# Quantizing a layer-normed tile: one int8 round trip replaced by an int32 conversion, its remainder and a correction

## The chip, the cores and the metric

The kernel runs on all 8 cores of one Trainium2 chip. Each core takes one of the eight sequences (2048 tokens of 1024 features) and does the whole layer on it; the cores exchange nothing. The metric is the device time of the slowest core, in microseconds.

## The reference, cut to what matters

One transformer layer with the norms behind the blocks: an attention block whose weights are 1 + s + s²/2 under a causal mask, normalised by their sum, a residual and a layer norm, and then a linear layer that quantizes its input by row:

```
x = layernorm(x + attn(x, Wq, Wk, Wv, Wo))
amax    = max(|x|, axis=-1);  x_scale = max(amax, 1e-6) / 127
x_q     = clip(round(x / x_scale), -128, 127)            # int8
acc     = x_q @ weight_q.T                               # int32
out     = acc * x_scale * weight_scale + bias
x = layernorm(x + out)
```

The part of this document is the line that makes x_q.

## The kernel before, in words

The program is written by hand as one instruction stream per engine, in program order: a wait list, the instruction, a semaphore increment. Each engine runs its stream in order, so the order of the loops in the code is the order on the engine.

The stages of a core, one behind the other:

- Projections. TensorE makes q, k and v from the transposed input and the weights (L235, L289), VectorE moves them out of PSUM (L248, L298).
- Attention, by pairs of heads: TensorE's scores (L442), ScalarE's square (L462), VectorE's added half and mask (L470 to L485), TensorE's product with v (L505), and the division by the row sums (L375, L394).
- Output projection, residual and statistics, by 16 tiles of 128 tokens (L597 to L620). The result stays in SBUF as `x1`, 128 x (16 * 1024) f32; mean, variance, minimum and maximum of each token go to small columns of `stat`. A run of small VectorE operations turns them into `S2` and `MM2`, the factor and offset that take a row of `x1` to quantized units, and `V1` and `NMR`, which take it to the layer norm's output.
- Quantization, a loop over the 16 tiles, the stage that the diff touches. Per tile:
  - VectorE: `mk1` (L702) writes `t6 = x1 * S2 + MM2` in f32; `mk2a` (L709) copies it to `xq8`, int8, which rounds it; `mk2b` (L716) copies that to `xq`, f16. `t6`, `xq8` and `xq` have two buffers each. L709 waits for L702, L716 for L709 and for the transposes of two tiles before.
  - GpSimd: `mkxm` (L721) replaces the tile of `x1` by its normed value, and `mkx1b` (L736) adds the bias to it. L721 waits for this tile's L702, L736 for L721.
  - TensorE: eight 128x128 transposes (L746) of `xq` into PSUM, which wait for L716.
  - ScalarE: one copy (L756) of them into `xqT`.
- The quantized matmuls, a second loop over the 16 tiles: sixteen matmuls each (L777) on `xqT` and the weights, then VectorE's scaling (L788) and residual with row sum (L795), and ScalarE's sum of squares (L804). As the second loop stands behind the first in the program, TensorE's matmuls stand behind all its transposes, and L788 behind all of the quantization on VectorE.
- The second layer norm and the stores (L835), which use `t6` again as a staging buffer.

The rounding of the quantization happens in the conversion from f32 to an integer type; the integers are then carried as f16, in which they are exact.

Of the kernel before, what the change touches and what calls it, by code (L numbers as in the profile page):

```python
# [9 lines left out]
I8 = mybir.dt.int8  # L10
AF = mybir.ActivationFunctionType
ALU = mybir.AluOpType
# [4 lines left out]
D = 1024  # L17
# [10 lines left out]
MAGIC = 12582912.0  # L28
# [65 lines left out]
def build_nc(debug=False, _waits=None):  # L94
    if _waits is None:
        _waits = _collect_waits(debug)
    return _build_nc_inner(debug, _waits)


def _collect_waits(debug):  # L100
    nc, plan = _build_nc_inner(debug, {}, collect_only=True)
    return {k: sorted(v) for k, v in plan.waited.items()}


def _build_nc_inner(debug, _waits, collect_only=False):
    nc = bass.Bass("TRN2", target_bir_lowering=False,
                   dynamic_dma_scratch_size=8192)
# [33 lines left out]
    sDV = Sem(e(nc.semaphore("sDV")), "sDV")  # L141
# [44 lines left out]
    plan = Plan(nc, last_wait)  # L186
    plan.future_waits = _waits

    for dst, src in ((wsb, d_wsb), (biasb, d_biasb), (tri, d_tri),
                     (ident, d_ident), (ones2, d_ones2)):  # L190
        plan.op("sync", lambda sy, dst=dst, src=src: sy.dma_start(dst[:, :], src),
                incs=[(sIO, 16)])
# [8 lines left out]
    for fi in range(NCH):  # L201
# [3 lines left out]
                incs=[(sCa, 16)])  # L205
# [3 lines left out]
                incs=[(sCa, 16)])  # L209
# [9 lines left out]
    for proj in range(2):  # L219
        for c in range(NCH):  # L220
# [6 lines left out]
            for fi in range(NCH):  # L227
                waits = [(sCa, dma_after[(proj, fi)])]
                if prev in evac_dv:
                    waits.append((sDV, evac_dv[prev]))  # L230
                for qcc in range(QC):
# [5 lines left out]
                    incs = ()  # L237
                    if qcc == QC - 1 and (c == NCH - 1 or fi == NCH - 1):
                        incs = [(sPE, 1)]
                    plan.op("tensor", mk, waits=waits if qcc == 0 else (),  # L240
                            incs=incs)
# [5 lines left out]
            def mkev(v, ps=ps, dst=dst, scale=scale, c=c):  # L247
# [3 lines left out]
                    incs=[(sDV, 1)])  # L251
            evac_dv[(proj, c)] = sDV.n
        nxt = d_wkt if proj == 0 else d_wvt
        for fi in range(NCH):
# [4 lines left out]
                    waits=[(sPE, w_last_use[(proj, fi)])],  # L259
                    incs=[(sCa, 16)])  # L260
# [8 lines left out]
           for i in range(2)]  # L269

    plan.op("vector", lambda v: v.memset(vz_blocks[:, :, 64:65], 1.0),
            incs=[(sDV, 1)])

    v_evac = {}
    for t in range(NT):
# [6 lines left out]
        for fi in range(NCH):  # L282
            waits = [(sCa, dma_after[(2, fi)])] + extra
            extra = []
            for half in range(2):
# [5 lines left out]
                incs = [(sPE, 1)] if (fi == NCH - 1 and half == 1) else ()  # L291
                plan.op("tensor", mk, waits=waits if half == 0 else (), incs=incs)
                waits = ()
# [9 lines left out]
    if debug:  # L303
        plan.op("sync", lambda sy: sy.dma_start(d_qto, qT[:, :]),
                waits=[(sDV, n_qk_evac)], incs=[(sIO, 16)])
        plan.op("sync", lambda sy: sy.dma_start(d_kto, kT[:, :]),
                waits=[(sDV, n_qk_evac)], incs=[(sIO, 16)])
        plan.op("sync", lambda sy: sy.dma_start(d_vzo, vz[:, :]),
                waits=[(sDV, n_vz_done)], incs=[(sIO, 16)])
# [18 lines left out]
    for fi in range(NCH):  # L328
# [4 lines left out]
                incs=[(sCa, 16)])  # L333
# [80 lines left out]
    for p in range(NP):  # L414
# [128 lines left out]
        if p > 0:  # L543
# [3 lines left out]
                waits=wio, incs=[(sIO, 16)])  # L547
        gather_done[p] = sIO.n
        if debug and p == 0:
            plan.op("sync", lambda sy: sy.dma_start(d_oso, ot_sb[0][:, :]),  # L550
                    incs=[(sIO, 16)])
# [20 lines left out]
    if debug:  # L572
        plan.op("sync", lambda sy: sy.dma_start(d_oto, ot_fin[:, :]),
                waits=list(w_all), incs=[(sIO, 16)])

    r1_done = {}
    for t in range(NT):
        wio = []
        if t >= 2:
            wio.append((sDV, r1_done[t - 2]))  # L580
        plan.op("sync",
                lambda sy, t=t: sy.dma_start(xstream[t % 2][:, :],
                                             d_xtok[t * 128:(t + 1) * 128, :]),
                waits=wio, incs=[(sIO, 16)])
# [7 lines left out]
        for fi in range(NCH):  # L592
            for half in range(2):
# [5 lines left out]
                incs = [(sPE, 1)] if (fi == NCH - 1 and half == 1) else ()  # L599
# [11 lines left out]
        def mksq1(s, t=t):  # L611
# [3 lines left out]
                incs=[(sSc, 1)])  # L615
# [3 lines left out]
        def mkmn(v, t=t):  # L619
# [6 lines left out]
            waits=[(sDV, r1_done[NT - 1])], incs=[(sDV, 1)])  # L626
    plan.op("vector", lambda v: v.tensor_scalar(V1, SQ1, INV1024, None, ALU.mult),
            waits=[(sSc, n_sq1)], incs=[(sDV, 1)])
    plan.op("vector", lambda v: v.tensor_tensor(MSQ, M1, M1, ALU.mult),
            waits=[(sDV, sDV.n)], incs=[(sDV, 1)])  # L630
    plan.op("vector", lambda v: v.tensor_tensor(V1, V1, MSQ, ALU.subtract),
            waits=[(sDV, sDV.n)], incs=[(sDV, 1)])
    plan.op("scalar", lambda s: s.activation(V1, V1, AF.Sqrt, bias=c_eps),
            waits=[(sDV, sDV.n)], incs=[(sSc, 1)])
    plan.op("vector", lambda v: v.reciprocal(V1, V1),
            waits=[(sSc, sSc.n)], incs=[(sDV, 1)])
# [3 lines left out]
            waits=[(sDV, n_rstd1)], incs=[(sDV, 1)])  # L640
    plan.op("vector", lambda v: v.tensor_tensor(MN, M1, MN, ALU.subtract),
            waits=[(sDV, sDV.n)], incs=[(sDV, 1)])
    plan.op("vector", lambda v: v.tensor_tensor(MX, MX, MN, ALU.max),
            waits=[(sDV, sDV.n)], incs=[(sDV, 1)])
    plan.op("vector", lambda v: v.tensor_tensor(AM, MX, V1, ALU.mult),
            waits=[(sDV, sDV.n)], incs=[(sDV, 1)])
    plan.op("vector",
            lambda v: v.tensor_scalar(XS, AM, 1e-6, INV127, ALU.max, ALU.mult),
            waits=[(sDV, sDV.n)], incs=[(sDV, 1)])
    plan.op("vector", lambda v: v.reciprocal(RQ, XS),  # L650
            waits=[(sDV, sDV.n)], incs=[(sDV, 1)])
    plan.op("vector", lambda v: v.tensor_tensor(S2, V1, RQ, ALU.mult),
            waits=[(sDV, sDV.n)], incs=[(sDV, 1)])
    plan.op("vector", lambda v: v.tensor_tensor(MM2, M1, S2, ALU.mult),
            waits=[(sDV, sDV.n)], incs=[(sDV, 1)])
    plan.op("vector",
            lambda v: v.tensor_scalar(MM2, MM2, -1.0, None, ALU.mult),
            waits=[(sDV, sDV.n)], incs=[(sDV, 1)])
    plan.op("vector", lambda v: v.tensor_tensor(NMR, M1, V1, ALU.mult),
            waits=[(sDV, sDV.n)], incs=[(sDV, 1)])  # L660
    plan.op("vector",
            lambda v: v.tensor_scalar(NMR, NMR, -1.0, None, ALU.mult),
            waits=[(sDV, sDV.n)], incs=[(sDV, 1)])
# [5 lines left out]
    ef = scope_f.enter_context  # L669
    wqf = ef(nc.sbuf_tensor("wqf", [128, NCH * D], F16))  # L670
    xqT = ef(nc.sbuf_tensor("xqT", [128, NCH * T], F16))
    xq = [ef(nc.sbuf_tensor(f"xq{i}", [128, D], F16)) for i in range(2)]
    t6 = [ef(nc.sbuf_tensor(f"t6{i}", [128, D], F32)) for i in range(2)]
    xq8 = [ef(nc.sbuf_tensor(f"xq8{i}", [128, D], I8)) for i in range(2)]
    t3 = [ef(nc.sbuf_tensor(f"t3{i}", [128, D], F32)) for i in range(2)]

    ph4_psum = contextlib.ExitStack()
# [5 lines left out]
    for fi in range(NCH):  # L683
# [3 lines left out]
                waits=[(sDV, div_done[NP - 1]), (sIO, obmove_done[NP - 1])]  # L687
                if fi == 0 else (),
                incs=[(sCa, 16)])
    n_wq = sCa.n  # L690

    rnd1_done = {}
# [4 lines left out]
    for t in range(NT):  # L697
        wv = [(sDV, n_qscale)]
        if t >= 2:
            wv.append((sDV, rnd2_done[t - 2]))  # L700
        def mk1(v, t=t):
            return v.tensor_scalar(t6[t % 2][:, :], x1[:, t * D:(t + 1) * D],  # L702
                                   S2[:, t:t + 1], MM2[:, t:t + 1],
                                   ALU.mult, ALU.add)
        plan.op("vector", mk1, waits=wv, incs=[(sDV, 1)])
        rnd1_done[t] = sDV.n

        def mk2a(v, t=t):
            return v.tensor_copy(xq8[t % 2][:, :], t6[t % 2][:, :])  # L709
        plan.op("vector", mk2a, waits=[(sDV, rnd1_done[t]), (sDV, sDV.n)],  # L710
                incs=[(sDV, 1)])
        wv = [(sDV, sDV.n)]
        if t >= 2:
            wv.append((sPE, tr_done[t - 2]))
        def mk2b(v, t=t):
            return v.tensor_copy(xq[t % 2][:, :], xq8[t % 2][:, :])  # L716
        plan.op("vector", mk2b, waits=wv, incs=[(sDV, 1)])
        rnd2_done[t] = sDV.n

        def mkxm(g, t=t):  # L720
            return g.tensor_scalar(x1[:, t * D:(t + 1) * D],  # L721
                                   x1[:, t * D:(t + 1) * D],
                                   V1[:, t:t + 1], NMR[:, t:t + 1],
                                   ALU.mult, ALU.add)
        plan.op("gpsimd", mkxm, waits=[(sDV, rnd1_done[t])], incs=[(sPo, 1)])
        n_xm = (sPo, sPo.n)
        if debug:
            plan.op("sync",
                    lambda sy, t=t: sy.dma_start(d_x1o[t * 128:(t + 1) * 128, :],
                                                 x1[:, t * D:(t + 1) * D]),  # L730
                    waits=[n_xm], incs=[(sIO, 16)])
        wx1b = [n_xm, (sIO, n_const)]
        if debug:
            wx1b.append((sIO, sIO.n))
        def mkx1b(g, t=t):
            return g.tensor_tensor(x1[:, t * D:(t + 1) * D],  # L736
                                   x1[:, t * D:(t + 1) * D], biasb[:, :], ALU.add)
        plan.op("gpsimd", mkx1b, waits=wx1b, incs=[(sPo, 1)])
        x1b_done[t] = sPo.n

        wpe = [(sDV, rnd2_done[t]), (sIO, n_const)]
        if t >= 2:
            wpe.append((sSc, trevac_done[t - 2]))
        for c in range(NCH):
            def mktr(tt, t=t, c=c):
                return tt.transpose(pst[t % 2][:, c * 128:(c + 1) * 128],  # L746
                                    xq[t % 2][:, c * 128:(c + 1) * 128],
                                    ident[:, :])
            plan.op("tensor", mktr, waits=wpe if c == 0 else (),
                    incs=[(sPE, 1)] if c == NCH - 1 else ())  # L750
            wpe = ()
        tr_done[t] = sPE.n
        def mktre(s, t=t):
            src = pst[t % 2].rearrange("p (c b) -> p c b", b=128)
            dst = xqT.rearrange("p (c u) -> p c u", u=T)[:, :, t * 128:(t + 1) * 128]
            return s.copy(dst, src)  # L756
        plan.op("scalar", mktre, waits=[(sPE, tr_done[t])], incs=[(sSc, 1)])
        trevac_done[t] = sSc.n

    if debug:  # L760
        plan.op("sync", lambda sy: sy.dma_start(d_xqo, xqT[:, :]),
                waits=[(sSc, trevac_done[NT - 1])], incs=[(sIO, 16)])
# [3 lines left out]
    for t in range(NT):  # L766
# [5 lines left out]
        for fi in range(NCH):  # L772
            for half in range(2):
# [5 lines left out]
                incs = [(sPE, 1)] if (fi == NCH - 1 and half == 1) else ()  # L779
# [14 lines left out]
        def mkr2(v, t=t):  # L794
# [5 lines left out]
                incs=[(sDV, 1)])  # L800
        r2_done[t] = sDV.n

        def mksq2(s, t=t):
# [3 lines left out]
                incs=[(sSc, 1)])  # L807
    n_sq2 = sSc.n

    if debug:  # L810
        plan.op("sync", lambda sy: sy.dma_start(d_r2o, x1[:, :]),
                waits=[(sDV, r2_done[NT - 1])], incs=[(sIO, 16)])

    plan.op("vector", lambda v: v.tensor_scalar(M1, S1, INV1024, None, ALU.mult),
            waits=[(sDV, r2_done[NT - 1])], incs=[(sDV, 1)])
    plan.op("vector", lambda v: v.tensor_scalar(V1, SQ1, INV1024, None, ALU.mult),
            waits=[(sSc, n_sq2)], incs=[(sDV, 1)])
    plan.op("vector", lambda v: v.tensor_tensor(MSQ, M1, M1, ALU.mult),
            waits=[(sDV, sDV.n)], incs=[(sDV, 1)])
    plan.op("vector", lambda v: v.tensor_tensor(V1, V1, MSQ, ALU.subtract),  # L820
            waits=[(sDV, sDV.n)], incs=[(sDV, 1)])
    plan.op("scalar", lambda s: s.activation(V1, V1, AF.Sqrt, bias=c_eps),
            waits=[(sDV, sDV.n)], incs=[(sSc, 1)])
    plan.op("vector", lambda v: v.reciprocal(V1, V1),
            waits=[(sSc, sSc.n)], incs=[(sDV, 1)])
# [4 lines left out]
    for t in range(NT):  # L830
# [3 lines left out]
        def mka2(v, t=t):  # L834
# [6 lines left out]
                lambda sy, t=t: sy.dma_start(d_out[t * 128:(t + 1) * 128, :],  # L841
                                             ostage[t % 4][:, :]),
                waits=[(sDV, na)], incs=[(sIO, 16)])
# [56 lines left out]
```

How the kernel before makes its waits and increments, by code:

```python
        def thunk(eng, wl=wl, builder=builder, incs=tuple(incs)):  # L74
            for s, v in wl:
                eng.wait_ge(s.h, v)
            inst = builder(eng)
            for s, k in incs:
                inst = inst.then_inc(s.h, k)
```

## Time and profile before

| | us |
|---|---|
| median of 13 runs | 946.97 |
| lowest and highest of them | 944.14, 982.76 |
| the profiled execution, its own time | 949.38 |
| its span on the slowest core (core 3) | 947.8 |
| spans of the eight cores | 931.6 to 947.8 |
| busy in that span: TensorE matmul | 617.3 |
| VectorE | 480.4 |
| ScalarE | 376.3 |
| GpSimd | 102.5 |

The page is of one execution, on its slowest core. The time is measured from outside and is a little longer than the span from first to last instruction. In the trace PE is TensorE, DVE is VectorE, ACT is ScalarE, POOL is GpSimd and SP the engine that issues most transfers. A line such as L702 is the line in the kernel that issued the instruction. Tensors are shown without their buffer numbers, and without digits at the end of their names: `t6` and `t3` are both t, `x1` is x, and `xq8` and `xq` both read xq, so that the line number tells them apart. The duration of an instruction in the records runs from its start to its end and can hold time in which it was held up.

### The profile page before, as it was taken

The page shows a single profiled execution, that of the slowest core. Times are in us where ns is not written, and L with a number is a line of the kernel's source. Part 1 is how long each engine was busy: PE and PEld are TensorE (multiplying, and loading weights), DVE is VectorE, ACT ScalarE, POOL GpSimd, SP SyncE. Part 2 cuts the span into 40 slices and gives each one's busy share as a digit, 9 for nine tenths or more (in the row PEclk, how much of TensorE's full clock was granted, in tenths as well). Part 3 has the DMA queues.
Part 4 walks back from the last instruction along what each step waited for, and adds up shares of the span by engine and source line. Part 5 has one row for each costly group of instructions (what it writes and reads, how often), then busy time and mean ns, then how long its engine had stood idle before and what let it go on. Part 6 is the DMA issues. An engine that isn't in the chain of part 4 may idle for free.

```text
span 947.8 us, 8730 instructions; the slowest of 8 cores (931.6 to 947.8 us)
## 1 busy us (share of the span) xinstructions
PE 617.3 (65%) x2688; PEld 222.2 (23%) x2688; DVE 480.4 (51%) x761; ACT 376.3 (40%) x403; POOL 102.5 (11%) x100
## 2 busy tenths in 40 slices
PE   1239948945997787878787778787089611259900
PEld 0014413411442221212222222222034211124400
DVE  0002202221334566665656665656359999967742
ACT  0000000000008987978797979788013311213300
POOL 1100010012000000000000000000010078850000
PEclk9999968975998989988989988889589955569955
DMA  6550040035100011110111110101164300000035
GB/s 113 101 98 1 12 66 12 1 56 87 35 1 1 0 25 34 25 34 24 34 25 34 25 34 24 34 25 34 46 192 152 111 1 0 0 1 1 0 133 221
DMA packets 14831, 43.87 MB, mean 46 GB/s; under 512 B 2244, under 2 KB 2756, under 8 KB 13764
## 3 DMA queue, kind: packets, MB, share of 16 engines
q0 software_dynamic: 8192, 23.07, 12.7%
q1 hardware_dynamic: 6596, 20.25, 6.5%
q8 instruction: 23, 0.38, 0.2%
q14 instruction: 20, 0.16, 0.1%
HBM read 44.11 MB, written 8.52 MB: 56 GB/s over the span
## 4 chain that ended last, share of the span: by engine, by line
PE 34%; DMA 23%; DVE 17%; ACT 15%; issue 9%; POOL 0%; DVEq 0%; ACTq 0%; POOLq 0%; SPq 0%
ACT uab L462 15%; PE pq L235 10%; PE oab L505 8%; PE pa L777 6%; DMA wbuf<-wqt 6%; PE pv L289 6%; DMA xs<-x_tok 6%; DVE t L702 4%; PE ps L442 4%; DMA wbuf<-wvt 3%; DMA wbuf<-wkt 3%; DVE xq L716 2%; DVE uab L470 2%; DVE ot_fin L375 2%; DMA out<-xs 2%
## 5 line engine op out<-in xcount | busy, mean ns | idle before, releaser
L462 ACT ACTIVATE uab<-ps,consts 128x1024 f16<-128x1024 f32 (+1 forms) x320 | 321.4, 1085 | 55.5 <-PE ps L442 55.5
L505 PE MATMUL oab<-uab,vz 128*65 128x512 f16 (+3 forms) x640 | 194.2, 388 | 62.4 <-DVE uab L485 31.3
L235 PE MATMUL pq<-xTsb,wbuf 128*128 128x512 f16 x512 | 127.6, 412 | 70.5 <-DMA wbuf<-wqt 53.6
L442 PE MATMUL ps<-qT,kT 64*128 64x512 f16 (+3 forms) x640 | 124.7, 386 | 22.9 <-ACT uab L462 20.9
L485 DVE TENSOR_SCALAR uab<-uab 128x1024 f16<-128x1024 f16 x192 | 79.4, 422 | 105.0 <-ACT uab L462 105.0
L462 ACT ACT_TABLE_LOAD x1 | 1.3, 1283 | 284.4 <-PE ps L442 284.4
L235 PEld LDWEIGHTS pq<-xTsb,wbuf 128*128 128x128 f16 x512 | 51.5, 103 | 146.1 <-issue 94.7
L505 PEld LDWEIGHTS oab<-uab,vz 128*65 128x65 f16 x640 | 48.1, 116 | 144.1 <-issue 143.2
L597 PE MATMUL py<-woT,ot_fin 128*128 128x512 f16 x256 | 59.3, 389 | 27.5 <-DMA ot_fin<-ob_tmp 25.6
L289 PE MATMUL pv<-wbuf,xTsb 128*128 128x512 f16 x256 | 61.0, 400 | 23.3 <-DMA wbuf<-wvt 20.8
L470 DVE SCALAR_TENSOR_TENSOR uab<-uab,tri_sb 128x256 f16<-128x256 f16 x128 | 54.5, 426 | 42.6 <-ACT uab L462 41.1
L442 PEld LDWEIGHTS ps<-qT,kT 64*128 64x128 f16 x640 | 34.8, 94 | 154.4 <-issue 153.7
L248 DVE TENSOR_SCALAR qT<-pq 128x2048 f16<-128x2048 f32 x8 | 18.3, 2292 | 101.6 <-PE pq L235 101.6
L746 PE MATMUL pt<-ident_sb,xq 128*128 128x128 f16 x128 | 16.2, 307 | 76.2 <-DVE xq L716 76.2
L777 PE MATMUL pa<-wqf,xqT 128*128 128x512 f16 x256 | 57.6, 389 | 0.0
L298 DVE CAST vz<-pv 128x1024 f16<-128x1024 f32 x16 | 19.6, 1225 | 62.5 <-PE pv L289 62.5
L248 DVE TENSOR_SCALAR kT<-pq 128x2048 f16<-128x2048 f32 x8 | 18.3, 2292 | 61.0 <-PE pq L235 61.0
L612 ACT ACTIVATE scratch<-x 128x1024 f32<-128x1024 f32 x16 | 16.9, 1058 | 74.1 <-DVE x L605 74.1
L756 ACT COPY xqT<-pt 128x1024 f16<-128x1024 f16 x16 | 16.2, 1013 | 70.3 <-PE pt L746 70.3
L702 DVE TENSOR_SCALAR t<-x,stat 128x1024 f32<-128x1024 f32 x16 | 43.2, 2698 | 0.1
L736 POOL TENSOR_TENSOR x<-x,biasb_sb 128x1024 f32<-128x1024 f32 x16 | 41.5, 2593 | 2.4
L524 DVE COPY otsb<-oab 65x1024 f32<-65x1024 f32 x32 | 38.9, 1214 | 4.2 <-PE oab L505 4.2
(63 smaller groups left out, 401.7 us busy)
## 6 DMA issues: line engine op xcount, KB each, us to landing
rzb<-rzscr POOLq DMA_DIRECT2D x16, 512.0 KB, 4.7
xs<-x_tok SPq DMA_DIRECT2D x16, 512.0 KB
xTsb<-xT POOLq DMA_DIRECT2D x8, 512.0 KB, 5.6
out<-xs SPq DMA_DIRECT2D x8, 512.0 KB
out<-t SPq DMA_DIRECT2D x8, 512.0 KB
wbuf<-wqt POOLq DMA_DIRECT2D x8, 256.0 KB, 6.3
wbuf<-wkt POOLq DMA_DIRECT2D x8, 256.0 KB, 3.6
wbuf<-wvt POOLq DMA_DIRECT2D x8, 256.0 KB, 3.6
```

Source lines behind the costliest of these rows:

```text
L235: return t.matmul(ps[:, qcc * 512:(qcc + 1) * 512], lhs, rhs, start=(fi == 0), stop=(fi == NCH - 1))
L289: return tt.matmul(ps[:, half * 512:(half + 1) * 512], lhs, rhs, start=(fi == 0), stop=(fi == NCH - 1))
L442: return t.matmul(ps[:, ab * 512 + js: ab * 512 + 512], lhs, rhs, start=True, stop=True, tile_position=(r0, 0))
L462: return s.activation(dst, src, AF.Square, bias=c_rs, scale=c_rs)
L470: return v.scalar_tensor_tensor(ub[:, :, js:js + 128], ub[:, :, js:js + 128], 0.5, tri[:, None, :].broadcast_to([128, 2, 128]), ALU.add, A ...
L485: return v.tensor_scalar(ub[:, :, :], ub[:, :, :], 0.5, None, ALU.add)
L505: return t.matmul(ob[0:65, ab * 512 + js: ab * 512 + 512], lhs, rhs, start=(kt == 0), stop=(kt == 4 * qc + 3))
L524: return v.tensor_copy(dst, src)
L597: return tt.matmul(ps[:, half * 512:(half + 1) * 512], lhs, rhs, start=(fi == 0), stop=(fi == NCH - 1))
L702: return v.tensor_scalar(t6[t % 2][:, :], x1[:, t * D:(t + 1) * D], S2[:, t:t + 1], MM2[:, t:t + 1], ALU.mult, ALU.add)
L736: return g.tensor_tensor(x1[:, t * D:(t + 1) * D], x1[:, t * D:(t + 1) * D], biasb[:, :], ALU.add)
L777: return tt.matmul(ps[:, half * 512:(half + 1) * 512], lhs, rhs, start=(fi == 0), stop=(fi == NCH - 1))
```

## The change

In the quantization loop `mk2a`, the copy from f32 to int8, goes, and five operations take its place; `mk2b` becomes an addition. `mkc` converts `t6` to int32 (`xq32`). `mke` subtracts that integer from `t6`, in place, which leaves the remainder. `mkm1` and `mkm2` add a large constant to the remainder and take it off again, two separate operations in f32, which rounds it to a whole number. `mkg` doubles that and writes it as int32 over the same bytes (`g32` is `t6` seen as int32). The new `mk2b` adds `xq32` and `g32` and writes the sum as f16. Each of the six waits for VectorE's semaphore count of the one before it; the wait for the transposes of two tiles before stays at `mk2b`. The buffer `xq8` (2 x 1 KB per partition) becomes `xq32` (2 x 4 KB). The streams of the other engines are not edited, and the bounds of the int8 type no longer clip.

```
+    xq32 = [ef(nc.sbuf_tensor(f"xq32{i}", [128, D], mybir.dt.int32))
+            for i in range(2)]
+    er = t6
+    g32 = [b[:, :].bitcast(mybir.dt.int32) for b in er]
...
-        def mk2a(v, t=t):
-            return v.tensor_copy(xq8[t % 2][:, :], t6[t % 2][:, :])
-        plan.op("vector", mk2a, waits=[(sDV, rnd1_done[t]), (sDV, sDV.n)],
+        def mkc(v, t=t):
+            return v.tensor_copy(xq32[t % 2][:, :], t6[t % 2][:, :])
+        plan.op("vector", mkc, waits=[(sDV, rnd1_done[t]), (sDV, sDV.n)],
                 incs=[(sDV, 1)])
+        def mke(v, t=t):
+            return v.tensor_tensor(t6[t % 2][:, :], t6[t % 2][:, :],
+                                   xq32[t % 2][:, :], ALU.subtract)
+        plan.op("vector", mke, waits=[(sDV, sDV.n)], incs=[(sDV, 1)])
+        def mkm1(v, t=t):
+            return v.tensor_scalar(er[t % 2][:, :], er[t % 2][:, :],
+                                   MAGIC, None, ALU.add)
+        plan.op("vector", mkm1, waits=[(sDV, sDV.n)], incs=[(sDV, 1)])
+        def mkm2(v, t=t):
+            return v.tensor_scalar(er[t % 2][:, :], er[t % 2][:, :],
+                                   -MAGIC, None, ALU.add)
+        plan.op("vector", mkm2, waits=[(sDV, sDV.n)], incs=[(sDV, 1)])
+        def mkg(v, t=t):
+            return v.tensor_scalar(g32[t % 2], er[t % 2][:, :],
+                                   2.0, None, ALU.mult)
+        plan.op("vector", mkg, waits=[(sDV, sDV.n)], incs=[(sDV, 1)])
...
         def mk2b(v, t=t):
-            return v.tensor_copy(xq[t % 2][:, :], xq8[t % 2][:, :])
+            return v.tensor_tensor(xq[t % 2][:, :], xq32[t % 2][:, :],
+                                   g32[t % 2], ALU.add)
```

## Rows read from the trace of the kernel before

**Rows 1.** The page's chain that ended last, its shares of the span by line.
```profile
ACT uab L462 15%; PE pq L235 10%; PE oab L505 8%; PE pa L777 6%; DMA wbuf<-wqt 6%; PE pv L289 6%; DMA xs<-x_tok 6%; DVE t L702 4%; PE ps L442 4%; DMA wbuf<-wvt 3%; DMA wbuf<-wkt 3%; DVE xq L716 2%; DVE uab L470 2%; DVE ot_fin L375 2%; DMA out<-xs 2%
```
**Rows 2.** The chain in order of time, 836 to 906 us: start, length, what.
```profile
840.09 1.45 DVE xq L716
...
841.78 1.01 PE pt L746 x8
842.80 57.44 PE pa L777 x256
```
**Rows 3.** Busy time by stretch: length, PE, PEld, DVE, ACT, POOL, clock, DMA share, GB/s.
```profile
761.00:842.80 81.80, 16.19 (x129) 12.61 (x130) 76.28 (x48) 15.20 (x15) 67.51 (x32) 0.50 0.00 1
842.80:860.00 17.20, 17.20 (x71) 7.35 (x70) 8.66 (x10) 4.47 (x7) 0.93 (x1) 0.88 0.00 0
```
**Rows 4.** TensorE by stretch, 842 to 854 us: length, busy, clock, DMA share, GB/s.
```profile
846.00:847.00 1.00, 1.00 (x4) 0.50 0.00 0
847.00:848.00 1.00, 1.00 (x6) 0.97 0.00 0
```
**Rows 5.** The timeline, the first tiles of quantization: start, duration, engine, line.
```profile
761.00 0.81 DVE L702 TENSOR_SCALAR t<-x,stat 128x1024 f32<-128x1024 f32 x1
...
764.14 2.82 DVE L702 TENSOR_SCALAR t<-x,stat 128x1024 f32<-128x1024 f32 x1
...
767.07 0.69 DVE L709 CAST xq<-t 128x1024 int8<-128x1024 f32 x1
767.14 1.69 POOL L721 TENSOR_SCALAR x<-x,stat 128x1024 f32<-128x1024 f32 x1 [0.73 <-DVE t L702]
767.86 1.51 DVE L716 CAST xq<-xq 128x1024 f16<-128x1024 int8 x1
768.98 2.59 POOL L736 TENSOR_TENSOR x<-x,biasb_sb 128x1024 f32<-128x1024 f32 x1
769.29 2.82 DVE L702 TENSOR_SCALAR t<-x,stat 128x1024 f32<-128x1024 f32 x1
...
773.09 1.44 DVE L716 CAST xq<-xq 128x1024 f16<-128x1024 int8 x1 [0.17 <-DVE xq L709]
```
**Rows 6.** Instructions of line L716: count, then shortest, median, longest duration in ns.
```profile
L716 DVE CAST xq<-xq x16: 1437/1441/1509, 762.7 to 840.1; 128x1024 f16<-128x1024 int8 x16
```
**Rows 7.** Groups by line and shape, 640 to 948 us: count, busy us, mean ns.
```profile
L709 DVE CAST xq<-t 128x1024 int8<-128x1024 f32 x16 | 11.1, 694 | 1.6
L375 DVE TENSOR_TENSOR ot_fin<-otsb,rzb 64x512 f16<-64x512 f32 x8 | 5.0, 678 | 7.3 <-DMA rzb<-rzscr 7.3
L795 DVE SCALAR_TENSOR_TENSOR x<-t,x 128x1024 f32<-128x1024 f32 x16 | 19.6, 1226 | 2.8 <-DVE t L788 2.8
L485 DVE TENSOR_SCALAR uab<-uab 128x1024 f16<-128x1024 f16 x12 | 4.8, 419 | 6.3 <-ACT uab L462 6.3
```
**Rows 8.** Waits, 761 to 843 us: us in total, times, longest.
```profile
PE pt L746 <- DVE xq L716: 76.2, 16, 14.0
POOL x L721 <- DVE t L702: 72.0, 16, 61.1
```
**Rows 9.** The page's costliest groups, two of VectorE's that read PSUM.
```profile
L248 DVE TENSOR_SCALAR qT<-pq 128x2048 f16<-128x2048 f32 x8 | 18.3, 2292 | 101.6 <-PE pq L235 101.6
...
L298 DVE CAST vz<-pv 128x1024 f16<-128x1024 f32 x16 | 19.6, 1225 | 62.5 <-PE pv L289 62.5
```
**Rows 10.** The timeline, the last tile of quantization and the first residual.
```profile
836.30 2.82 DVE L702 TENSOR_SCALAR t<-x,stat 128x1024 f32<-128x1024 f32 x1
...
840.09 1.44 DVE L716 CAST xq<-xq 128x1024 f16<-128x1024 int8 x1 [0.17 <-DVE xq L709]
841.13 2.60 POOL L736 TENSOR_TENSOR x<-x,biasb_sb 128x1024 f32<-128x1024 f32 x1
...
850.00 1.23 DVE L795 SCALAR_TENSOR_TENSOR x<-t,x 128x1024 f32<-128x1024 f32 x1 [0.17 <-DVE t L788]
```
**Rows 11.** Spans and mean granted clock of two cores, the slowest and the fastest.
```profile
core 2: 931.6 us, clock 0.843
core 3: 947.8 us, clock 0.841
```

More of the change, by code:

```diff
@@ L673, in _build_nc_inner @@
     t6 = [ef(nc.sbuf_tensor(f"t6{i}", [128, D], F32)) for i in range(2)]
-    xq8 = [ef(nc.sbuf_tensor(f"xq8{i}", [128, D], I8)) for i in range(2)]
+    xq32 = [ef(nc.sbuf_tensor(f"xq32{i}", [128, D], mybir.dt.int32))
+            for i in range(2)]
+    er = t6
+    g32 = [b[:, :].bitcast(mybir.dt.int32) for b in er]
     t3 = [ef(nc.sbuf_tensor(f"t3{i}", [128, D], F32)) for i in range(2)]
```

## The prediction

> **What bounds the kernel now.** I read the chain of waits first. It is the view that says which work sets the end, and its list by line gives the line of the tile being quantized (L702) 4% of the span, and the cast after it (L716) 2% [rows 1]. The chain in order of time around the stage's end shows how they stand to the rest: the last cast ends at 841.54 us, eight transposes follow at once, and then 57.44 us of matmuls (L777) without a gap [rows 2]. In the program TensorE gets all sixteen tiles' transposes before the first matmul of L777, so no matmul of that group can start before the last tile is quantized. Whatever the quantizing loop gains or loses is gained or lost by the end.
>
> Then I asked for busy time by stretch. From 761.0 to 842.8 us VectorE is busy 76.28 of 81.80 us and GpSimd 67.51, TensorE only 16.19, at a granted clock of 0.50, the lower of its two levels, 1.2 GHz [rows 3]. The list of waits says the same from the other side: TensorE stands 76.2 us in this stage waiting for L716 [rows 8]. Inside the matmul group the clock is at 0.50 until about 847 us and then at full speed, 2.4 GHz [rows 4].
>
> "VectorE is busy" is not yet the answer, and the timeline of one tile shows why. L702 takes 0.81 us for the first tile and 2.82 us for every later one; L716 takes 1.51 or 1.44 us, though L709, an operation of the same size before it, takes 0.69 [rows 5, 6]. Put the ends beside each other. L709 ends at 767.76 us, and GpSimd's L721, recorded from 767.14, ends 1.07 us after that, at 768.83. VectorE's L716, recorded from 767.86, ends at 769.37, 0.54 us after L721. GpSimd's L736 ends at 771.57, 2.20 us after L716; VectorE's next L702, recorded from 769.29, ends at 772.11, 0.54 us after L736 [rows 5]. So the two engines take turns: in each pair the later one is held until the earlier one has ended, and its recorded time holds that wait. The tile's period, 5.15 us, is the sum of five operations of two engines, and about 2.9 us of it is VectorE held by GpSimd (2.82 - 0.81 = 2.01 and 1.51 - 0.69 = 0.82).
>
> **The change, part by part.** Per tile two VectorE operations (L709, L716) go and six come: mkc (f32 to int32), mke (two tensors), mkm1, mkm2, mkg (one tensor each, 4-byte), mk2b (two int32 tensors to f16). L702 stays, and so do GpSimd's two operations, which start on L702's end [rows 8].
>
> The prices. mkc, mkm1, mkm2 and mkg are one-tensor operations over 128x1024 without a scalar per partition: I take L709's 0.694 us [rows 7]. One that was held ends about 0.55 us after its release, so 0.15 us of its record is start-up that the wait hides. For two tensors of 4 bytes, L375 has 678 ns for 512 columns [rows 7]; the step from 1024 to 2048 columns where VectorE takes one column at a time is (2292 - 1225) / 1024 = 1.04 ns per column [rows 9]; 0.678 + 512 x 0.00104 = 1.21 us, and L795, also two tensors in, has 1.23 [rows 7]. mke and mk2b get 1.21, or 1.06 when released from a wait. Between operations that wait for their predecessor lie 0.11 us (L702's end at 766.96 to 767.07), sometimes 0.17 [rows 5]. L702 starts 0.08 us before the end of the operation in front of it (769.29 against 769.37) [rows 5].
>
> No row shows a two-tensor VectorE operation beside a GpSimd one: L795 starts only after GpSimd's last operation has ended (850.00 against 841.13 + 2.60 us) [rows 10]. This is the unknown that matters, since mke stands just where L721 runs. From below: it runs beside GpSimd and costs its bare 1.21. From above: it is held like the two operations that the rows show held. I take the upper end, because the nearest rows are the VectorE operations of this very loop, and each that met a GpSimd operation waited to its end, as GpSimd did the other way round [rows 5, 10].
>
> On that point the Trainium skill ("SBUF — State Buffer", Who interferes with whom) says that VectorE and GpSimd share a pair of ports as an exclusive lock, that the first to start keeps it for its whole instruction, and that an operation with two SBUF inputs contends with a GpSimd operation that reads SBUF although it has no two-port mode. By that rule the sum is the one below; had the rule named the two-port modes alone, it would be the first rival's. The rows show the lock for one-tensor operations only.
>
> One tile after the change, from L702's end at 0, in us:
> - mkc 0.11 to 0.80. L721 comes at 0.18, is held to 0.80 and runs its 1.07 to 1.87.
> - mke is held to 1.87 and ends at 2.93. L736 comes at 2.02 (0.15 after L721, as 768.98 against 768.83), is held, and runs its 2.20 to 5.13.
> - mkm1 is held to 5.13 and ends at 5.68. GpSimd now has nothing more for this tile.
> - mkm2 to 6.48, mkg to 7.28, mk2b (0.11 + 1.21) to 8.60; the next L702 from 8.52 to 9.33, not held any more.
>
> The period goes from 5.15 to 9.33, by 4.17 us unrounded. Fifteen periods: 62.6 us. The last tile ends 8.60 after its L702, where it was 841.53 - 839.12 = 2.41 [rows 10]: 6.2 us more. Sum: 68.8 us. As a second way: two casts of 0.69 go, two operations of 1.21 and four of 0.69 come, with four gaps more: +4.2 a tile. GpSimd's 3.27 us are in the path before and after, only behind other operations.
>
> What I cost at nothing: the transposes (1.01 us) and ScalarE's copy of a tile lie in TensorE's wait, which grows; without that cover they would add 2 us once. GpSimd's result of a tile is wanted by L795 in the next stage alone. Each added operation waits for VectorE's own semaphore; behind it stand the rest of the tile, then this tile's transposes, and through the last tile the matmuls. No DMA is added or moved, SP's and GpSimd's queues keep their contents. The clock is at 0.50 in the whole stage already and the matmuls start on it already, so I leave their 57.44 us.
>
> The profiled execution has a span of 947.8 us and a time of 949.4 us; 949.4 + 68.8 = 1018.2. The median of the runs shown, 946.97, is 2.4 below the profiled one: **1015.8 us**, which I forecast as 1016. All cores run the same loop, so the slowest stays the slowest [rows 11]. Its own bounds: gaps of 0.17 in place of 0.11 at five places add 4.8 us, start-ups that aren't hidden 16 x 2 x 0.15 = 4.8 more; releases 0.1 us earlier at two places a tile take off 3: 1013 to 1025.
>
> **The rivals** (times by the median).
> - *mke runs beside GpSimd.* Then mke ends at 2.12, under L721; L736 runs from 2.02 to 4.22; mkm1 ends at 4.77, mk2b at 7.69, the next L702 at 8.42. Period 8.42: 15 x 3.27 + 5.28 = 54.3, so 1001 us. For it: mke takes a column per step, unlike the operations seen held. Against it: no row with any overlap.
> - *GpSimd no longer stands in the way*, because GpSimd's operations fall beside VectorE's everywhere. Then VectorE's operations alone make 0.73 + 0.80 + 1.32 + 3 x 0.80 + 1.32 = 6.57 a tile, 15 x 1.42 + 3.4 = 24.7, so 972. Against it: L721 and L736 still start on L702's end, amid one-tensor operations, and these were held [rows 5].
> - *Integer forms are dearer.* If mkc and mkg go one column per step (1.21, not 0.69), 16 x 2 x 0.52 = 16.6 more: 1032. If also each of mke and mk2b read their two tensors one after the other, they cost as much as L248's 2048 columns, 2.29 us [rows 9], 34.5 more on the forecast: 1050 alone. L709, which writes an integer type at 0.69, speaks against the first.
> - *Not slower.* The mechanism: the added operations run at the rate of L485, 0.42 us for 128x1024 [rows 7] (two tensors at 0.69), so that VectorE gets through its own seven operations while GpSimd has its turns beside them. The chain is then 0.73 + 0.53 + 0.80 + 3 x 0.53 + 0.80 = 4.45 a tile: 15 x (-0.70) + 1.3 = -9, so 938. It decides from a chain of 5.03 us a tile. Against it: L485 works on 2-byte data, every tensor added here but the last output is of 4 bytes, and L709's 0.69 and L702's free 0.81 are what 4-byte rows cost [rows 5, 7].
>
> **How the numbers follow.** The forecast has 0.60, mke beside GpSimd 0.24, dearer integer forms 0.09 (0.06 the first, 0.03 the second), no GpSimd in the way 0.04, not slower 0.01; 0.02 remain for what I don't see. The range 998 to 1027 holds the first two with their gaps, 0.84, and leaves the rest out. A change under 0.3% is what a measurement here can't tell from none; every case but the last and half of the unseen is far above it: slower 0.98, same 0.01, faster 0.01.
>
> **What would show it.** In the changed profile L721 should be recorded at about 1.69 us and L736 at about 3.1 (held by mke) rather than 2.59; mke at about 2.0 us and mkm1 at about 2.45 to 2.6, both mostly wait; mkm2, mkg at 0.69; mk2b at 1.21; L702 at 0.81 throughout. The period would be 9.3 us and the stage some 150 us, with the same 57 us of matmuls behind it and VectorE's lines of this loop at some 15% of the chain. If mke is recorded at 1.21 it ran beside L721, and the first rival holds. If the period is under 7 us or the matmuls start before the last tile's transposes, the reading of the stage is wrong.

## The result, and the profile after

The changed kernel takes 1016.09 us (median of 11 runs) against 946.6 (48 runs); the ratio is 1.0731, 95% interval 1.0713 to 1.0750. The forecast was 1016. The profiled execution took 1017.18 us with a span of 1015.7. Some executions of either kernel fell in a slower state, with a lower granted clock on some of the cores (982.76 us before, 1053.96 after); the ratio leaves them out.

The chain of waits of the changed kernel, in order of time around the stage's end (start, length, what), answers to [rows 2]:

```profile
908.52 1.24 DVE xq L735
...
910.00 1.01 PE pt L766 x8
911.01 57.10 PE pa L797 x256
```

The order is as before: the last tile's last VectorE operation, its transposes, and the matmuls in one piece, 57.10 us against 57.44. The stage in front of them, from L702 (now L705), took 841.5 - 761.0 = 80.5 us; now it takes 909.8 - 759.0 = 150.8. That is 70.3 us, and the medians differ by 69.5: the whole change lies here. The stage has the same length, to 0.1 us, on all eight cores, in both profiled executions. (The slowest core entered the stage 2 us earlier this time, so the two profiled executions differ by 67.8.)

Busy time by stretch of the changed kernel (length, PE, PEld, DVE, ACT, POOL, clock, DMA share, GB/s), beside [rows 3]:

```profile
759.00:909.80 150.80, 15.17 (x120) 11.61 (x120) 139.36 (x112) 15.18 (x15) 76.83 (x32) 0.50 0.00 0
911.00:968.20 57.20, 57.10 (x257) 25.25 (x254) 37.76 (x45) 17.71 (x30) 0.00 (x0) 0.97 0.00 1
```

TensorE's clock is 0.50, 1.2 GHz, all through the stage, and the matmuls have 0.97 on average (0.96 before): nothing moved there.

The timeline of the second tile, VectorE first and then GpSimd (start, duration, engine, line), with the start of the third tile; it answers to [rows 5]:

```profile
768.32 0.81 DVE L705 TENSOR_SCALAR t<-x,stat 128x1024 f32<-128x1024 f32 x1
769.23 0.69 DVE L712 CAST xq<-t 128x1024 int32<-128x1024 f32 x1
770.03 2.03 DVE L716 TENSOR_TENSOR t<-t,xq 128x1024 f32<-128x1024 f32 x1
772.17 2.64 DVE L720 TENSOR_SCALAR t<-t 128x1024 f32<-128x1024 f32 x1
774.91 0.69 DVE L724 TENSOR_SCALAR t<-t 128x1024 f32<-128x1024 f32 x1
775.71 0.69 DVE L728 TENSOR_SCALAR t<-t 128x1024 int32<-128x1024 f32 x1
776.51 1.23 DVE L735 TENSOR_TENSOR xq<-xq,t 128x1024 f16<-128x1024 int32 x1
777.65 0.81 DVE L705 TENSOR_SCALAR t<-x,stat 128x1024 f32<-128x1024 f32 x1
...
785.91 1.23 DVE L735 TENSOR_TENSOR xq<-xq,t 128x1024 f16<-128x1024 int32 x1 [0.17 <-DVE t L728]
...
769.31 1.69 POOL L741 TENSOR_SCALAR x<-x,stat 128x1024 f32<-128x1024 f32 x1 [4.38 <-DVE t L705]
771.14 3.12 POOL L756 TENSOR_TENSOR x<-x,biasb_sb 128x1024 f32<-128x1024 f32 x1
```

Read it as a relay. mkc (L712) ends at 769.92; GpSimd's L741, recorded from 769.31, ends at 771.00, 1.08 us after. mke (L716), recorded from 770.03, ends at 772.06, 1.06 after L741. L756 ends at 774.26, 2.20 after mke, and mkm1 (L720) at 774.81, 0.55 after L756. From there to the next tile VectorE is alone and nothing is held: L705 is at 0.81 us, where L702 stood at 2.82. The holds have moved from L716 and L702 to mke and mkm1.

### The profile page after: what moved, and what is told of

Same layout as the page of the kernel before. It is cut to its first block, busy times and chain, and to the rows that moved or that the text cites. A ratio compares the mean times of both kernels' runs of the same rounds, so it can differ in the third digit from the quotient of the medians.

```text
span 1015.7 us, 8858 instructions; the slowest of 8 cores (1004.8 to 1015.7 us)
## 1 busy us (share of the span) xinstructions
PE 618.9 (61%) x2688; PEld 222.3 (22%) x2688; DVE 543.5 (54%) x825; ACT 376.0 (37%) x403; POOL 110.8 (11%) x100
## 4 chain that ended last, share of the span: by engine, by line
PE 32%; DVE 22%; DMA 21%; ACT 14%; issue 9%; POOL 0%; DVEq 0%; ACTq 0%; POOLq 0%; SPq 0%
ACT uab L462 14%; PE pq L235 9%; PE oab L505 7%; PE pa L797 6%; DMA wbuf<-wqt 6%; PE pv L289 5%; DMA xs<-x_tok 5%; DVE t L720 4%; PE ps L442 4%; DVE t L716 3%; DMA wbuf<-wvt 3%; DMA wbuf<-wkt 3%; DVE xq L735 2%; DVE ot_fin L375 2%; DVE uab L470 2%
## 5 line engine op out<-in xcount | busy, mean ns | idle before, releaser
L756 POOL TENSOR_TENSOR x<-x,biasb_sb 128x1024 f32<-128x1024 f32 x16 | 49.9, 3118 | 2.4
L766 PEld LDWEIGHTS pt<-ident_sb,xq 128*128 128x128 f16 x128 | 12.4, 137 | 150.5 <-issue 150.5
L720 DVE TENSOR_SCALAR t<-t 128x1024 f32<-128x1024 f32 x16 | 42.3, 2642 | 1.7
```

The costliest lines, as they stand in the source:

```text
L720: return v.tensor_scalar(er[t % 2][:, :], er[t % 2][:, :], MAGIC, None, ALU.add)
L756: return g.tensor_tensor(x1[:, t * D:(t + 1) * D], x1[:, t * D:(t + 1) * D], biasb[:, :], ALU.add)
```

## The experiments

All are edits of the kernel before or of the changed one, timed beside the kernel before. Its median was 946.53 us beside four of them (the changed kernel without GpSimd's operations, the int32 copy, the one instruction, and the scaling on ScalarE in the changed kernel) and 946.27 beside the other four.

**The changed kernel without GpSimd's two operations.** Is mke held, or dear by itself? The edit (cut: the builders of the two operations go too, and the residual no longer waits for GpSimd):

```
-        plan.op("gpsimd", mkxm, waits=[(sDV, rnd1_done[t])], incs=[(sPo, 1)])
-        plan.op("gpsimd", mkx1b, waits=wx1b, incs=[(sPo, 1)])
```

> The changed kernel without GpSimd's two operations in the quantization loop (it leaves out the norm's scaling of the residual tile and the bias). Theory (VectorE and GpSimd take turns, and the new two-tensor subtraction is held like the others): with nothing to be held by, mke is recorded at 1.21 to 1.23 us instead of 2.03, mkm1 at 0.69 instead of 2.64, the period is 6.57 us instead of 9.40, the stage 105 us instead of 151, the time about 1016 - 46 = 970 us. Rival (mke is dear by itself, since it mixes f32 and int32): mke stays at 2.03, the period is 7.4 us, the time about 983 us.

Measured: 972.23 us, ratio to the kernel before 1.0278 [1.0229, 1.0326]. Its timeline, part of one tile and the next tile's start:

```profile
769.55 0.81 DVE L705 TENSOR_SCALAR t<-x,stat 128x1024 f32<-128x1024 f32 x1
...
771.25 1.23 DVE L716 TENSOR_TENSOR t<-t,xq 128x1024 f32<-128x1024 f32 x1
772.59 0.69 DVE L720 TENSOR_SCALAR t<-t 128x1024 f32<-128x1024 f32 x1
...
776.19 0.81 DVE L705 TENSOR_SCALAR t<-x,stat 128x1024 f32<-128x1024 f32 x1
```

and the first and the last line of its stage (count, then shortest, median, longest duration in ns, first and last start):

```profile
L705 DVE TENSOR_SCALAR t<-x,stat x16: 804/807/814, 756.4 to 856.4; 128x1024 f32<-128x1024 f32 x16
L735 DVE TENSOR_TENSOR xq<-xq,t x16: 1224/1226/1226, 761.8 to 861.9; 128x1024 f16<-128x1024 int32 x16
```

mke is 1.23 us with the same f32 and int32 tensors, mkm1 0.69, the period 6.64. So the 0.80 and 1.95 us more in the changed kernel are waits for GpSimd, and the rival falls.

**The kernel before without them.** The same edit.

> The kernel before without GpSimd's two operations in the quantization loop (it leaves out the norm's scaling of the residual tile and the bias). Theory (GpSimd's share of the path is the same before and after the change): L702 0.81, L709 and L716 0.69 us, period 2.33 us, stage 37 us instead of 80.5, time about 946.6 - 43 = 904 us, and the changed kernel without GpSimd 67 us above it. Rival (before, GpSimd's operations were partly hidden under VectorE, and the change only exposes them): the gain is clearly less than 40 us here and clearly more from the changed kernel.

Measured: 904.44 us, ratio 0.9553 [0.9503, 0.9602]. One period of its timeline, and the first and the last line of its stage:

```profile
776.14 0.81 DVE L702 TENSOR_SCALAR t<-x,stat 128x1024 f32<-128x1024 f32 x1
777.05 0.69 DVE L709 CAST xq<-t 128x1024 int8<-128x1024 f32 x1
777.92 0.69 DVE L716 CAST xq<-xq 128x1024 f16<-128x1024 int8 x1 [0.17 <-DVE xq L709]
778.53 0.81 DVE L702 TENSOR_SCALAR t<-x,stat 128x1024 f32<-128x1024 f32 x1
...
L702 DVE TENSOR_SCALAR t<-x,stat x16: 804/807/814, 759.6 to 795.2; 128x1024 f32<-128x1024 f32 x16
L716 DVE CAST xq<-xq x16: 693/694/695, 761.3 to 797.0; 128x1024 f16<-128x1024 int8 x16
```

L702's 2.82 us were 0.81 of work. Taken together: GpSimd costs 946.27 - 904.44 = 41.8 us before the change and 1016.09 - 972.23 = 43.9 after it; without GpSimd the change costs 972.23 - 904.44 = 67.8. These medians have intervals of about 5 us each. The stage is read more closely, from its first start to the end of its last operation: 797.0 + 0.69 - 759.6 = 38.1 us here and 861.9 + 1.23 - 756.4 = 106.7 in the run above, against 80.5 and 150.8 with GpSimd. So of the stage's 70.3 us, 68.6 are VectorE's own added work, bare, and 1.7 are GpSimd's: 42.4 us before the change and 44.1 after it.

**The int32 copy alone.** The kernel before, with one type changed:

```
-    xq8 = [ef(nc.sbuf_tensor(f"xq8{i}", [128, D], I8)) for i in range(2)]
+    xq32 = [ef(nc.sbuf_tensor(f"xq32{i}", [128, D], mybir.dt.int32)) for i in range(2)]
```

> The kernel before with the rounding copy to int32 instead of int8, and nothing else of the change. Theory (an integer output costs what its rows of 4-byte data cost, whatever its width): both casts keep their 0.69 us before waits, L702 2.82 and L716 1.44 us recorded, time the same as before within 0.3%. Rival (wider integers are dearer): one column per step, 1.21 us each, 16 x 2 x 0.52 = 17 us more, about 963 us.

Measured: 946.18 us, ratio 0.9996 [0.9972, 1.0020]. Its groups by line (count, busy us, mean ns, idle before):

```profile
L716 DVE CAST xq<-xq 128x1024 f16<-128x1024 int32 x16 | 23.2, 1449 | 2.6 <-DVE xq L709 2.4
...
L709 DVE CAST xq<-t 128x1024 int32<-128x1024 f32 x16 | 11.1, 694 | 1.6
```

L709 has the 694 ns of [rows 7] to the digit. The wider integer costs nothing, so dearer integer forms are out for the two copies; for mkg and the new mk2b they are out by the changed kernel's timeline (0.69 and 1.23 us).

**One instruction for the two additions.** The changed kernel with

```
+            return v.tensor_scalar(er[t % 2][:, :], er[t % 2][:, :],
+                                   MAGIC, -MAGIC, ALU.add, ALU.add)
```

in place of mkm1 and mkm2.

> The changed kernel with the two additions of the rounding constant in one instruction with two operations. Theory (each VectorE operation behind the held one lies bare on the path): one operation of 0.69 us and its gap of 0.11 go per tile, 16 x 0.80 = 12.8 us, about 1003 us. Rival (it is hidden beside GpSimd, which then holds the next one longer): no gain, 1016 us. Rival (two operations in one instruction take two passes): no gain either, but with the fused operation recorded at over 3 us.

Measured: 1002.57 us, ratio 1.0596 [1.0540, 1.0652]; 13.5 us below the changed kernel. Its groups by line, the fused operation (L720) and mke, and then, from the changed kernel, mkm1, which is L720 there:

```profile
L720 DVE TENSOR_SCALAR t<-t 128x1024 f32<-128x1024 f32 x16 | 42.3, 2642 | 1.7
L716 DVE TENSOR_TENSOR t<-t,xq 128x1024 f32<-128x1024 f32 x16 | 32.5, 2032 | 1.7
...
L720 DVE TENSOR_SCALAR t<-t x16: 2639/2642/2646, 762.8 to 904.1; 128x1024 f32<-128x1024 f32 x16
```

The fused operation is recorded at 2642 ns, as mkm1 alone was. An operation behind the held one lies bare on the path, and two arithmetic steps in one instruction cost one.

**The norm's scaling on ScalarE, in the changed kernel.** GpSimd's first operation of a tile goes to ScalarE, which copies only one transposed tile a period:

```
-        def mkxm(g, t=t):
-            return g.tensor_scalar(x1[:, t * D:(t + 1) * D],
...
+        def mkxm(s, t=t):
+            return s.activation(x1[:, t * D:(t + 1) * D],
+                                x1[:, t * D:(t + 1) * D], AF.Identity,
+                                bias=NMR[:, t:t + 1], scale=V1[:, t:t + 1])
```

> The changed kernel with the norm's scaling (GpSimd's first operation of a tile) on ScalarE; the bias stays on GpSimd. Theory: mke meets no GpSimd operation and is recorded at 1.21 to 1.23 us; one VectorE operation behind it is held by the bias (2.2 us); period 8.5 us, time about 1003 us. Rival (mke dear by itself): mke 2.03, time about 1012 us. Rival (moving work off GpSimd gains all of its 1.07 us and the lost start-ups): period 8.2, time about 997 us.

Measured: 1010.5 us, ratio 1.0692 [1.0631, 1.0753]: a miss by 7 us, nearest in time to the first rival. The timeline says it isn't that rival:

```profile
786.84 0.81 DVE L705 TENSOR_SCALAR t<-x,stat 128x1024 f32<-128x1024 f32 x1
...
788.55 1.23 DVE L716 TENSOR_TENSOR t<-t,xq 128x1024 f32<-128x1024 f32 x1
789.88 0.69 DVE L720 TENSOR_SCALAR t<-t 128x1024 f32<-128x1024 f32 x1
790.68 2.79 DVE L724 TENSOR_SCALAR t<-t 128x1024 f32<-128x1024 f32 x1
...
795.58 0.81 DVE L705 TENSOR_SCALAR t<-x,stat 128x1024 f32<-128x1024 f32 x1
...
790.58 2.34 POOL L755 TENSOR_TENSOR x<-x,biasb_sb 128x1024 f32<-128x1024 f32 x1 [6.41 <-ACT x L741]
```

mke is at its bare 1.23; the bias now comes 0.01 us after mkm1's end and holds mkm2. It runs 2.34 us and not 2.20; as I read it, because it waited for nothing under which its start-up could hide. The period is 795.58 - 786.84 = 8.74 us where 8.5 was expected: 0.14 of start-up and 0.07 of a longer gap (below). The stage of the slowest core is 139.8 us, 11.0 shorter than in the changed kernel, which makes 1005. The other 5 us of the median aren't in the stage, and their cause is open: the four runs spread from 1007.11 to 1021.07 us, and in the profiled one the slowest core entered the stage at 761.1 us, 2.1 later than in the changed kernel, and the earliest at 747.0. What sets that spread was not looked into.

**The same in the kernel before.**

> The kernel before with the norm's scaling on ScalarE, the bias on GpSimd as it was. Theory: one held VectorE operation a tile instead of two; period 4.35 to 4.4 us instead of 5.155, 12 to 13 us less, about 934 us. Rival (ScalarE's copy of the transposed tile, in order behind the scaling, becomes the bound): period about 5 us, no gain.

Measured: 933.99 us, ratio 0.9871 [0.9831, 0.9911]. The timeline, one tile (VectorE, then GpSimd):

```profile
779.39 2.83 DVE L702 TENSOR_SCALAR t<-x,stat 128x1024 f32<-128x1024 f32 x1
782.33 0.69 DVE L709 CAST xq<-t 128x1024 int8<-128x1024 f32 x1
783.19 0.69 DVE L716 CAST xq<-xq 128x1024 f16<-128x1024 int8 x1 [0.17 <-DVE xq L709]
783.80 2.83 DVE L702 TENSOR_SCALAR t<-x,stat 128x1024 f32<-128x1024 f32 x1
...
779.29 2.38 POOL L735 TENSOR_TENSOR x<-x,biasb_sb 128x1024 f32<-128x1024 f32 x1 [2.03 <-ACT x L721]
```

Period 4.41 us, as expected, so ScalarE isn't the bound; L716 is free at 0.69, L702 still held by the bias.

**The bias behind the whole quantization, in both kernels.** As the last two, and GpSimd's sixteen additions wait for the last tile, so that they fall beside the matmuls:

```
+    for t in range(NT):
+        def mkx1b(g, t=t):
...
+        plan.op("gpsimd", mkx1b,
+                waits=[xm_done[t], (sDV, rnd2_done[NT - 1]), (sIO, n_const)],
+                incs=[(sPo, 1)])
```

> The kernel before with the norm's scaling on ScalarE and GpSimd's sixteen bias additions placed behind the whole quantization, beside the matmuls. Theory (the lock costs only where VectorE is the bound): the stage shrinks from 80.5 to about 38 to 42 us; in the matmul stage VectorE's residual operation, with two tensors in SBUF, is held up to 2.2 us for some ten tiles, which costs about 10 us; about 917 us. Rival (ScalarE bounds the short stage): period over 3 us, about 930 us. Rival (the turns in the matmul stage cost what they cost before): about 945 us.

> The changed kernel with the same two moves. Theory: the period is VectorE's own 6.57 us, stage 105 us, matmul stage some 10 us longer; about 980 us. Rival (the turns cost the same in the matmul stage): about 1010 us.

Measured: 904.43 us on the kernel before, ratio 0.9561 [0.9525, 0.9596], the fastest kernel here that does all of the work; 972.22 on the changed one, 1.0280 [1.0241, 1.0318]. Both are what the kernels take without GpSimd (904.44, 972.23): the turns in the matmul stage cost nothing that these medians show, where I expected 10 us. Timeline of the first in its matmul stage, VectorE and then GpSimd:

```profile
807.17 1.27 DVE L793 SCALAR_TENSOR_TENSOR t<-pa,stat,wsb_sb 128x1024 f32<-128x1024 f32 x1
808.62 1.93 DVE L800 SCALAR_TENSOR_TENSOR x<-t,x 128x1024 f32<-128x1024 f32 x1 [0.17 <-DVE t L793]
...
810.48 1.27 DVE L793 SCALAR_TENSOR_TENSOR t<-pa,stat,wsb_sb 128x1024 f32<-128x1024 f32 x1
...
796.89 47.97 POOL L762 TENSOR_TENSOR x<-x,biasb_sb 128x1024 f32<-128x1024 f32 x16 [97.73 <-ACT xqT L752]
```

and its busy time by stretch:

```profile
758.60:796.80 38.20, 15.17 (x120) 11.61 (x120) 33.87 (x48) 32.30 (x31) 0.00 (x0) 0.50 0.00 1
798.00:854.80 56.80, 56.78 (x256) 25.20 (x254) 45.70 (x45) 17.62 (x31) 46.85 (x16) 0.97 0.00 1
```

The residual (L800, two tensors in SBUF) is held there too: 1.93 us, where L795 had 1.23 [rows 7]. L793, which reads PSUM and one tensor of SBUF, is not: 1.27 us with GpSimd busy beside it. So GpSimd's addition runs mostly under L793, and VectorE's period is 810.48 - 807.17 = 3.31 us, under TensorE's mean of 56.80 / 16 = 3.55. I had stacked the whole 2.2 us on VectorE's time. The first rival is out too: the quantization takes 38.20 us, as without GpSimd, though ScalarE is busy for 32.30 of it.

## Why the prediction was right

- **The stage is on the path as it stands.** Shown: the stage grew by 70.3 us, the time by 69.5, and the matmuls behind it kept their length.
- **The two engines take turns.** Shown by taking GpSimd away: every long record of the loop fell to its bare duration, in both kernels.
- **The unknown, mke beside GpSimd, at its upper end.** Shown: 2.03 us recorded beside L741, 1.23 without GpSimd, 1.23 with L741 on ScalarE; and L800 in another stage, 1.93 against 1.23, while L793, with one tensor in SBUF, is not held (1.27 us; 1.28 in the kernel before, where GpSimd idles beside it). The first rival (1001 us) is out by mke's record and by the time. The Trainium skill ("SBUF — State Buffer", Who interferes with whom) has the rule that two SBUF inputs contend with a GpSimd operation that reads SBUF; mke at 2.03 us agrees. Its other half is that an operation with one SBUF input outside the two-port modes doesn't contend; L793 at 1.27 us agrees.
- **Operation prices.** mkc, mkm2 and mkg at 0.69, mk2b at 1.23 for 1.21. Dearer integer forms: out, by mkg and mk2b's records and the int32 copy alone.
- **The period.** Worked out: 9.33. Measured: 777.65 - 768.32 = 9.33 for the second tile, 9.41 from the third on (787.06 - 777.65 in the same timeline). The sum was 68.8 and is 70.3. The longer gap before mk2b (0.17 for 0.11) makes 13 x 0.06 = 0.8, one still longer gap in the 15th tile (0.53) makes 0.4, and mk2b 16 x 0.016 = 0.25. The prediction's bounds had reckoned with such gaps at five places a tile; they came at one.
- **The last digit is luck.** 1016 against 1016.09 is closer than the parts: the stage grew by 1.5 us more than the sum, the base of 946.97 lay 0.4 above the median of all runs before, and most single executions of the changed kernel lie anywhere from 1013.37 to 1017.81.
- **GpSimd's share is nearly the same before and after.** 42.4 and 44.1 us of the stage. The 1.7 us between come from the last tile, and the prediction's sum has them: it lets a period grow by 4.17 us and the last tile by 6.2. Before, the last tile's bias addition (L736) runs from 841.13 to 843.73 us [rows 10], beside the transposes and matmuls, and holds nothing of the stage; after, it holds mkm1 in the last tile as in every other (2639 to 2646 ns for all sixteen).
- **GpSimd not in the way, and not slower.** The first is out by the holds on mke and mkm1 and by the time; its 972 us is what the changed kernel takes when GpSimd's operations are taken away (972.23). The second is out by the same run: even so the changed kernel is 2.8% slower, since VectorE's own chain is 6.64 us against a period of 5.15.

## What to carry to other kernels

Before pricing an added operation, look whether the engine's long records are work or waits: here 2.9 us of each 5.15 were VectorE waiting for GpSimd, and the added operations did not fill that wait, because the two engines run one behind the other. Put GpSimd's SBUF work where VectorE has slack or reads PSUM: the same sixteen additions cost 933.99 - 904.43 = 29.6 us beside the quantization and nothing measurable beside the matmuls. An operation on an engine that bounds its stage costs its full length and its gap, however small its part in the whole profile looks.

## What the runs showed of the hardware that was not expected

- The gap before the loop's last operation is 0.17 us, not 0.11, from the third tile on, where its second wait (the transposes of two tiles before, long done) joins the first. It is so before and after the change (2.4 and 2.8 us of idle time, 14 times; the 2.8 hold one gap of 0.53, in the 15th tile of the changed kernel, whose cause is open). That the second wait is the cause of the 0.17 was not tried by itself.
- A held operation is cheaper after its release than a free one: 0.55 us after it for 0.69, 1.06 for 1.23, and on GpSimd 2.20 for 2.34. Two engines in turns thus take less than the sum of their free durations. That start-up runs during the wait fits all three, and was not tried by itself.
- Two additions in one VectorE instruction cost what one costs (2642 ns recorded, wait and all, for both).
